# Inverse Fourier products as 64x64 quarters, in rounds behind pairs of convolution pieces, two groups ahead

## What is computed

```python
t = einsum('bchw,oc->bohw', x, w_in)
tf = rfft2(t in 8x8 patches) * fft_filter
t = irfft2(tf)                                  # the inverse products of the change
t = conv_general_dilated(t, w_dw, 'SAME', feature_group_count=192)
x1, x2 = t[:, :96], t[:, 96:]
return einsum('bchw,oc->bohw', gelu(x1) * x2, w_out)
```

## Time and profile before

| | us |
|---|---|
| median of 3 runs | 2518.32 (2510.87 to 2520.17) |
| the profiled execution, its own time | 2516.11 |
| its span in the trace | 2514.1 |
| middle stage of the first patch layer, in the trace | 184.44 to 291.29 |
| middle stage of the last patch layer, in the trace | 2324.11 to 2428.68 |

### The profile page before, as it was taken

One profiled execution on the slowest core, in us unless ns is written; L12 is line 12 of the kernel. 1 busy time (PEld: TensorE's weight loads), 2 busy tenths in 40 slices (PEclk: granted clock), 3 DMA queues, 4 the chain that ended last, 5 costly groups with the idle time before them and its releaser, 6 DMA issues. The chain is left out here.

```text
span 2514.1 us, 64417 instructions
## 1 busy us (share of the span) xinstructions
PE 2202.5 (88%) x23092; PEld 1626.4 (65%) x23092; DVE 1662.3 (66%) x3168; ACT 1304.1 (52%) x2719; POOL 1113.6 (44%) x1393
## 2 busy tenths in 40 slices
PE   0699988997899169999999999999996989969998
PEld 0565636786688137777777777777775756447563
DVE  5345575664565168888888888888883455834557
ACT  0355440174047247777777777777762555424544
POOL 0333250000000137788787787788772232533325
PEclk9999998999899579999999999999998999979999
DMA  8624495415523312222222222222225134961459
GB/s 210 178 79 85 126 316 140 108 34 190 177 51 122 115 35 58 59 61 56 59 60 56 59 60 56 59 60 56 60 49 169 51 77 103 332 182 51 85 125 318
DMA packets 305628, 272.25 MB, mean 108 GB/s; under 512 B 175966, under 2 KB 238846, under 8 KB 299210
## 3 DMA queue, kind: packets, MB, share of 16 engines
q1 hardware_dynamic: 294698, 256.00, 36.7%
q0 software_dynamic: 9280, 6.44, 2.1%
q10 hardware_dynamic: 1496, 7.63, 0.8%
HBM read 165.29 MB, written 81.46 MB: 98 GB/s over the span
## 5 line engine op out<-in xcount | busy, mean ns | idle before, releaser
L1669 DVE TENSOR_TENSOR l_scan_att<-l_scan_decay,l_scan_causal_scores 128x512 f32<-128x512 f32 x384 | 326.7, 851 | 64.3 <-ACT l_scan_decay L1638 64.0
L715 ACT COPY l_arena<-l_body_bank 128x384 f32<-128x384 f32 x192 | 142.0, 901 | 262.3 <-PE l_body_bank L587 262.3
L1632 ACT ACTIVATE l_scan_decay<-l_scan_cum 128x512 f32<-128x512 f32 x384 | 216.2, 597 | 32.7 <-PE l_scan_cum L1524 32.5
L1638 ACT ACTIVATE l_scan_decay<-l_scan_decay 128x512 f32<-128x512 f32 x384 | 227.8, 631 | 4.1
L1649 ACT ACTIVATE l_scan_yw<-l_scan_y_by_channel,l_scan_norm_b,l_scan_norm_w 128x128 f32<-128x128 f32 x384 | 148.0, 456 | 125.4 <-PE l_scan_y_by_channel L1586 124.4
L1571 PE MATMUL l_scan_gate_projected<-l_scan_xr,l_wf 97*128 97x128 f32 (+1 forms) x1536 | 205.3, 283 | 1.3 <-DVE l_scan_xo L1724 1.2
L1602 PE MATMUL l_scan_gate_projected<-l_scan_yz,l_scan_wo 128*96 128x128 f32 x1536 | 198.5, 279 | 1.1 <-DVE l_scan_yz L1701 1.1
L567 POOL TENSOR_TENSOR l_arena<-l_arena 96x512 f32<-96x512 f32 x96 | 122.7, 1279 | 167.8 <-ACT l_arena L780 160.3
L1602 PEld LDWEIGHTS l_scan_gate_projected<-l_scan_yz,l_scan_wo 128*96 128x96 f32 x1536 | 170.9, 163 | 40.0 <-issue 29.6
L1489 POOL TENSOR_TENSOR l_scan_inter<-l_scan_inter,l_scan_xd 128x384 f32<-128x384 f32 x128 | 128.0, 1000 | 150.7 <-DVE l_scan_inter L1684 150.7
L1571 PEld LDWEIGHTS l_scan_gate_projected<-l_scan_xr,l_wf 97*128 97x128 f32 (+1 forms) x1536 | 181.0, 190 | 17.2 <-issue 2.2
(11 more groups left out here) (193 smaller groups left out, 5064.8 us busy)
## 6 DMA issues: line engine op xcount, KB each, us to landing
l_scan_xc<-convolved_rows SPq DMA_DIRECT2D x128, 224.0 KB, 2.8
x_after<-l_arena SPq DMA_DIRECT2D x64, 384.0 KB, 5.0
l_arena<-x_after SPq DMA_DIRECT2D x64, 384.0 KB, 5.7
convolved_rows<-l_slots SPq DMA_DIRECT2D x48, 441.0 KB
l_conv_x_main<-x_after SPq DMA_DIRECT2D x64, 256.0 KB, 2.6
l_arena<-x_after SPq DMA_DIRECT2D x16, 1024.0 KB, 8.6
prepare_xt<-x SPq DMA_DIRECT2D x8, 1536.0 KB
l_arena<-x SPq DMA_DIRECT2D x32, 384.0 KB, 5.7
```

The lines of the kernel that those rows point to most:

```text
L715: nc.scalar.copy(tA[:, b, :, j:j + 2].rearrange("p c q -> p q c"), bank[n % 4][:, 0:2 * C].rearrange("p (q c) -> p q c", q=2)).then_inc(t_ ...
L1632: nc.scalar.activation(decay[:, b % 2, 4 * g:4 * g + 4, :], cum[(b + g) % 2][:], ACT.Relu, scale=-1.0)\
L1638: nc.scalar.activation(group, group, ACT.Exp, scale=-1.0).then_inc(exp_done, 1)
L1669: nc.vector.tensor_tensor(att[:, b, 4 * g:4 * g + 4, :], decay[:, b % 2, 4 * g:4 * g + 4, :], causal[:, b % 2:b % 2 + 1, :].broadcast_to([ ...
```

## The change

`invert` works by quarters, as `transform` does. A round is four products of 64x64 by 512 columns: one for each half of the channels (the quarter's rows) and for even and odd slabs (its columns). A round returns four channels of each half, so three rounds make a group in place of six products; it fills banks 2 and 3 both, and the next round waits until the four copies of the round before are done. Each engine still copies twice per round and six times per group, 64 partitions by 512 elements, now as 4 channels by 8 rows by 16: VectorE those of the even slabs, ScalarE those of the odd ones.

Round q of group g+2 now stands behind pieces 2q and 2q+1 of `convolve(g)`; the copies are spread over VectorE's and ScalarE's lists in the same way. Only groups 0 and 1 are inverted ahead of the loop. There are still three strips. The rings are issued as before, each behind the last copy of its group.

```diff
@@ -617,23 +617,26 @@
                                                     bands[:, g * n_row:(g + 1) * n_row], start=True, stop=True)
                         last.then_inc(built, 1)
 
-                def invert(g):
-                    for p in range(PIECES):
-                        n = g * PIECES + p
-                        if n >= 2:
-                            pe.wait_ge(own_top, n - 1)
-                            pe.wait_ge(own_low, n - 1)
-                        c = g * PAIR + 2 * p
-                        nc.tensor.matmul(bank[2 + n % 2][:], idft, freq[:, c:c + 2, :].rearrange("p c n -> p (c n)"),
-                                         start=True, stop=True).then_inc(back, 1)
-
-                def convolve(g):
+                def invert(g, rounds=range(PIECES // 2)):
+                    for q in rounds:
+                        n = g * PIECES // 2 + q
+                        if n >= 1:
+                            pe.wait_ge(own_top, 2 * n)
+                            pe.wait_ge(own_low, 2 * n)
+                        for h in range(2):
+                            for c in range(2):
+                                at, first = slice(64 * c, 64 * c + 64), g * PAIR + 4 * q
+                                last = nc.tensor.matmul(bank[2 + c][64 * h:64 * h + 64, :], idft[at, at],
+                                                        by_slab[at, first:first + 4, :, h, :], start=True, stop=True)
+                        last.then_inc(back, 1)
+
+                def convolve(g, pieces):
                     b = g % STRIPS
                     pe.wait_ge(ringed[b], 16 * RING_SIDES * (g // STRIPS + 1))
                     pe.wait_ge(cornered[b], 16 * (len(ring_strips()) - RING_SIDES) * (g // STRIPS + 1))
                     pe.wait_ge(mats_even, 2 * (g + 1))
                     pe.wait_ge(mats_odd, 2 * (g + 1))
-                    for p in range(PIECES):
+                    for p in pieces:
                         n = g * PIECES + p
                         if n >= 4:
                             og, op = divmod(n - 4, PIECES)
@@ -661,16 +664,16 @@
                 build(0, 0)
                 invert(1)
                 build(0, 1)
-                invert(2)
                 build(1, 0)
                 for g in range(groups):
-                    convolve(g)
-                    if g + 1 < groups:
-                        build(g + 1, 1)
-                    if g + 3 < groups:
-                        invert(g + 3)
-                    if g + 2 < groups:
-                        build(g + 2, 0)
+                    for q in range(PIECES // 2):
+                        convolve(g, [2 * q, 2 * q + 1])
+                        if g + 2 < groups:
+                            invert(g + 2, [q])
+                        if q == 1 and g + 1 < groups:
+                            build(g + 1, 1)
+                        if q == 2 and g + 2 < groups:
+                            build(g + 2, 0)
 
                 def turn(i):
                     for f in range(4):
@@ -729,17 +732,18 @@
                     nc.scalar.copy(mats[:, g % 2, :, 16 * f:16 * (f + 1)].rearrange("p c m -> p m c"),
                                    bank[n % 2][0:WIN, 0:16 * GROUP_CH].rearrange("p (m c) -> p m c", m=16)).then_inc(mats_odd, 1)
 
-                def place(g):
+                def place(g, rounds=range(PIECES // 2)):
                     if g >= STRIPS:
                         act.wait_ge(convolved, PIECES * (g - STRIPS + 1))
-                    for p in range(PIECES):
-                        n = g * PIECES + p
-                        act.wait_ge(back, n + 1)
-                        nc.scalar.copy(win[g % STRIPS][0:64, PAIR + 2 * p:PAIR + 2 * p + 2, 0:NPC, 0:NPC],
-                                       bank[2 + n % 2][64:128, :].rearrange("p (c i j) -> p c i j", c=2, i=NPC)).then_inc(own_low, 1)
-
-                def gelu(g):
-                    for p in range(3):
+                    for q in rounds:
+                        act.wait_ge(back, g * PIECES // 2 + q + 1)
+                        for c in range(2):
+                            first = PAIR * c + 4 * q
+                            nc.scalar.copy(win[g % STRIPS][0:64, first:first + 4, 1:NPC:2, 0:NPC],
+                                           bank[2 + c][64:128, :].rearrange("p (c i j) -> p c i j", c=4, i=slabs)).then_inc(own_low, 1)
+
+                def gelu(g, pieces):
+                    for p in pieces:
                         n = g * PIECES + p
                         act.wait_ge(convolved, n + 1)
                         c = g * PAIR + 4 * p
@@ -750,15 +754,18 @@
                 matrices(0, 1)
                 place(1)
                 matrices(0, 3)
-                place(2)
                 matrices(1, 1)
                 for g in range(groups):
-                    gelu(g)
+                    gelu(g, [0])
+                    if g + 2 < groups:
+                        place(g + 2, [0])
+                    gelu(g, [1, 2])
+                    if g + 2 < groups:
+                        place(g + 2, [1])
                     if g + 1 < groups:
                         matrices(g + 1, 3)
-                    if g + 3 < groups:
-                        place(g + 3)
                     if g + 2 < groups:
+                        place(g + 2, [2])
                         matrices(g + 2, 1)
 
                 def gather(i):
@@ -824,18 +831,19 @@
                                           bank[n % 2][0:WIN, 0:16 * GROUP_CH].rearrange("p (m c) -> p m c", m=16))\
                         .then_inc(mats_even, 1)
 
-                def place(g):
+                def place(g, rounds=range(PIECES // 2)):
                     if g >= STRIPS:
                         dve.wait_ge(convolved, PIECES * (g - STRIPS + 1))
-                    for p in range(PIECES):
-                        n = g * PIECES + p
-                        dve.wait_ge(back, n + 1)
-                        nc.vector.tensor_copy(win[g % STRIPS][0:64, 2 * p:2 * p + 2, 0:NPC, 0:NPC],
-                                              bank[2 + n % 2][0:64, :].rearrange("p (c i j) -> p c i j", c=2, i=NPC))\
-                            .then_inc(own_top, 1)
-
-                def gate(g):
-                    for p in range(3):
+                    for q in rounds:
+                        dve.wait_ge(back, g * PIECES // 2 + q + 1)
+                        for c in range(2):
+                            first = PAIR * c + 4 * q
+                            nc.vector.tensor_copy(win[g % STRIPS][0:64, first:first + 4, 0:NPC:2, 0:NPC],
+                                                  bank[2 + c][0:64, :].rearrange("p (c i j) -> p c i j", c=4, i=slabs))\
+                                .then_inc(own_top, 1)
+
+                def gate(g, pieces):
+                    for p in pieces:
                         n = g * PIECES + 3 + p
                         dve.wait_ge(convolved, n + 1)
                         dve.wait_ge(gelu_done, 3 * g + p + 1)
@@ -848,14 +856,19 @@
                 matrices(0, 0)
                 place(1)
                 matrices(0, 2)
-                place(2)
                 matrices(1, 0)
                 for g in range(groups):
-                    gate(g)
+                    if g + 2 < groups:
+                        place(g + 2, [0])
+                    gate(g, [0])
+                    if g + 2 < groups:
+                        place(g + 2, [1])
                     if g + 1 < groups:
                         matrices(g + 1, 2)
-                    if g + 3 < groups:
-                        place(g + 3)
+                    gate(g, [1])
+                    if g + 2 < groups:
+                        place(g + 2, [2])
+                    gate(g, [2])
                     if g + 2 < groups:
                         matrices(g + 2, 0)
 
```

## The result

The changed kernel takes 2528.09 us (median of 20 runs, 2517.38 to 2542.64) against 2511.12 us (median of 20, 2503.49 to 2520.17) for the kernel before on the same chip. The ratio is 1.0066, with a 95% interval of 1.005 to 1.0083: **slower by 0.66%, 17 us**. The predicted 2522 us is 6 us too low. Most of that closeness is luck: the three runs that were shown of the kernel before had a median of 2518.32, 7 us above that of the 20, so against its own baseline the forecast of +4 us was 13 us short.

The account below looks back on a forecast made before the run. TensorE's work was taken to bound the steady part, with ring waits taking over after the change. A net +1.3 us in each of three layers, +4 us on 2516.1, gave 2520, stated as 2522; range 2490 to 2544.

Parts of the forecast that it names:

- The mechanism: Middle stages: TensorE's work falls from 11.96 to 9.3 us a group, then ring waits bind at 10.85 a group.
- quarters overlap four at a time: Inverse products: four quarters cost one full product, 0.97 us a round; the rival without overlap, 2640 us, had 0.02.
- The start: Inversion ahead of the loop: ring 0 lands and `convolve(0)` starts at 203.5 in place of 208.4, 4.9 us earlier.
- The group of rounds: Ahead of the loop, where nothing covers the copies: 2.7 us a round, 8.0 a group in place of 6.1.
- the mean of 11.1: Time of a ring of DMAs from first issue until traffic ends, averaged over five rings of 10.2 to 12.2 us.
- Changing the array's form: TensorE switching between convolution, quarters and full width, eight times a group in place of two: taken as 0.
- The loop: From `convolve(g)` through inversion and copies of g+2, 10.6 us, then its ring, 11.1, to `convolve(g+2)`: 21.7 for two groups.
- the even chain: Starts of `convolve` for groups 0, 2, 4, 6, linked by rings: 21.7 us a link, plus clock losses.
- The forecast fall of 1.7 us: Idle time of 3 or 4 us in every second group lets the granted clock fall, costing 1.7 us.
- My sum: First layer's `convolve` starts added up to an end at 292.6 against 291.3: +1.3 us, taken for three layers, +4.
- The clock staying up: Rival: no clock falls at the steady idle gaps, 5.2 us earlier per layer, 2503 us; chance 0.20.
- fall in both chains at every wait: Rival: clock falls cost 2.6 us more on each link of both chains, 6.7 us later per layer, 2538; chance 0.26.

Follow-up runs that it names:

- e3: The changed kernel with rings cut to 6 of 12 channel pairs from group 3 on; 2501.35 us (one run).
- e9: The changed kernel with all ten DMAs of a ring issued by SP, none by GpSimd; 2546.69 us, ratio 1.0128 to the kernel before.
- e4: The changed kernel with small unread products after each round of groups 0 and 1 and ahead of `convolve(0)`; 2530.65 us, ratio 1.0053 to the kernel before.
- e2: The changed kernel with the full 128x128 products of before, two to a round, in place of quarters; 2570.33 us (one run).
- e8: The changed kernel with unread products at the start, as in e4, and ahead of groups 2, 4 and 6; 2526.98 us, ratio 1.0032 to the kernel before.
- e10: The changed kernel with each round ahead of its pieces, and unread products at the start and ahead of `convolve(7)`; 2492.46 us, ratio 0.9908 to the kernel before.

## Why the prediction was right and wrong

**The mechanism was right.** TensorE's products were the bound, the change takes them from there, and the ring with one group's time in place of two takes over: the ring waits rose from 14.9 to 35.9 us in three layers. In the first layer they are 11.9 (2.08 + 2.16 + 4.38 + 2.73 + 0.57), in place of 5.7; I had given 15 to 25, with groups of 9.3 us of work where they have 9.8, so that less of each ring's time shows as waiting; the place is right and the size too large. The lead is given back at the end, as forecast: c7 comes 3.9 us later than before. e3 and e9 show that it is the ring. That quarters overlap four at a time was right too.

**The start was mis-sized**, by 3.9 us: `convolve(0)` was forecast 19.1 us after the first product and came at 23.0. Two terms of that step failed. The group of rounds, forecast at 8.0 us, ended at 9.2, because the clock fell already after the first round, when TensorE had been busy 1.09 of 3.40 us; I had it low only in group 1's rounds. And ring 0 took 13.8 us in place of the mean of 11.1: I averaged rings whose lengths are not scattered about a mean but come in two kinds, which the windows of the kernel before show (10.1, 12.1, 12.2, 10.7 and 10.2 us for groups 3 to 7, two of them in the earlier trace rows). Ring 0 itself had a time there that I did not use: SP issued it at 190.99, 17.4 us ahead of `convolve(0)`, with ring 1 only 7.1 us behind. That the next ring follows later did help, as I had thought, but not down to 11.1: 17.4 us with the next ring 7.1 behind it, 15.2 with 8.0 (e4), 13.8 with 10.1. So the start gained 0.9 us on the kernel before, not the 4.9 I put ahead of the loop's losses.

**Changing the array's form was put at 0 and costs some 0.5 us a group.** e3 and the undisturbed groups of the change take 9.8 us where the parts add up to 9.3: from start to start a pair of pieces takes 1.96 in place of 1.86, a round 1.02 in place of 0.97, a build 0.43 in place of 0.34 or 0.43. There are eight changes in a group where the kernel before has two, so that is 0.09 us for each of the six more, and over 24 groups 12 us of TensorE, not all of it on the path. e2 agrees: four more changes than before, and a group of 12.3 us in place of 11.96, 0.08 each. That it is the change itself, and not another cost of the finer order, was not taken apart.

The rows could have shown it; I compared unlike times. The forward unit's 5.75 us of the earlier trace rows run from its start to the next one's (98.41 to 104.16), while the 5.76 of six full products is a duration with its tail. From start to start those take 5.61 (216.89 to 222.50 in the earlier trace rows), so three changes came with 0.14 us more, not with none.

The Trainium skill (TensorEngine Tiling, Key Properties) says that a change of tiling mode drains the array. The Trainium skill (TensorE: Matmul & The Clock Gate, Step-by-step: what each phase is for) gives the drain of a product as some 128 cycles; as an estimate that is 0.053 us for a change at full clock. The measurement is on the side of the page, at 0.05 us in the forward unit and 0.08 to 0.09 in the middle stage, and I had set it aside.

**The loop** was close. Two groups of the even chain took 24.1 and 24.9 us in the first layer, from `convolve(2)` on, where 23.4 was forecast; of the odd one 21.8, 26.5 and 21.0 where it was 21.7, 25.1 and 21.7. The forecast fall of 1.7 us is in the rows: it cost 2.5 at 258.01 (5.46 to the second pair in place of 2.98) and 1.6 at 282.89 (5.44 for 64 instructions in place of 3.83). That the long rings are those of groups 4 and 5 makes the fall at `convolve(4)` certain rather than likely; each of the three layers has its wait of 4.2 to 4.6 us there.

**One layer was taken for three.** My sum gave +1.3 us for the first and multiplied. They were +3.9, +4.8 and +5.9: the last one was 104.6 before, 2.3 shorter than the first, because `convolve(0)` waited 1.5 us less for its ring and the clock was low for 3.4 us in place of 6.8. The change brings all three to the same 111, with the same five waits in each. The row of the last layer stood there to be used.

**The rivals.** The clock staying up did not happen, nor did it fall in both chains at every wait, which would have cost 6.7 us per layer: the odd groups wait only at the end. The outcome lies between my forecast and that rival, at 4.9 per layer, just over the 4.2 from which I had said slower is decided. Rhythm, waits and clock are those of the main forecast. The first layer ended 2.6 us later than the sum had it: 3.9 from the start and 1.7 from the way between `convolve(0)` and `convolve(7)` (82.1 us in place of 80.4), less 3.1 behind it, where the sum held 1.7 for a fall of the clock that did not come and the 1.4 of handoffs that belong to the loop. So the mis-sized start took it over the line. "Slower" had 0.32 where "within 0.5%" had 0.40.

## What to carry to other kernels

When a change takes work from the engine that bounds a loop, draw the loop that comes next, product to copy to transfer to product, and price each of its links by the row of that very link (the ring of that group, the round without its cover) and not by a mean over all. Give the transfer more lead before you take out more work: moving each round ahead of its pair turned +17 us into -10. And where an engine waits a known time for a transfer and is dense afterwards, work that nobody reads may be worth putting into the wait, if it lasts until the transfer lands: 20 small products gave 11 us to the kernel before, and eight that ended 3.7 us early gave nothing to the changed one.

## What the runs showed of the hardware

- In the changed kernel a ring of ten DMAs takes, by its place in the layer, 9.7 to 11.5 us (groups 2, 3, 6, 7) or 13 to 14 (groups 0, 1, 4, 5), in all three layers. In the long ones SP's issues of four DMAs take 6.3 to 7.3 us in place of 3.1 to 3.2; those of ring 2 take 3.16 in the first layer and 4.8 and 4.7 in the others, though it stays short. With all ten on SP (e9) every ring that was waited for took some 13 us or more, up to 14.4. The place is not all: ring 7 took 14.2 us once in e8 and 13.3 once in e10. What holds SP up, and why by group, was not settled.
- A change of the array's form comes with 0.08 to 0.09 us more of TensorE in the middle stage (9.8 us a group where the parts add up to 9.3, with six changes more; 12.3 in place of 11.96 in e2, with four more).
- The granted clock fell to 0.51 2.0 us after the start of the first quarter round, with TensorE busy 1.09 of 3.40 us, and stayed low for 27.3 us, into the second pair of `convolve(0)`; in the other two layers it fell 1.4 to 1.6 us after that start and was low as long. With idle products in the gaps it did not fall until the wait of 3.66 us (e4), and with the wait filled it did not fall at all in the first two stages (e10). The Trainium skill (TensorE: Matmul & The Clock Gate, HAM oscillation — how this bites in real kernels) tells of such falls in waits for DMAs between bursts; the trace agrees at 256.50 and 283.8. The fall at 188.20 came between bursts too, but with copies waited for and no DMA.
